# Square roots and rows of a first routing moved from GpSimd and VectorE to ScalarE, and two index layouts cut into smaller pieces

## The reference

```python
x = x + 0.5 * ffn(layernorm(x))          # first mixture of experts
x = x + attention(layernorm(x))          # 16 heads of 8 features, queries = keys = values
x = x + 0.5 * ffn(layernorm(x))          # second mixture, same weights

def ffn(x):                              # 8 experts, 128 -> 512 -> 128, two per token
    xf = layernorm(x) * ln_g + ln_b
    scores, idx = top_k(xf @ router_w, 2)
    gate = softmax(scores)
    # per expert: h = layernorm(xf) * eg + eb
    #             y = clip((h @ W1 + b1) * silu(clip(h @ W2 + b2))) @ Wo + bo
    return sum of gate * expert(xf)
```

## Time and profile before

| | us |
|---|---|
| median of 3 runs (1407.98, 1411.99, 3628.1) | 1411.99 |
| the profiled execution, its own time | 1400.55 |
| its span, from the first to the last instruction | 1398.8 |
| PE busy | 1254.7 (90%) |
| DVE busy | 1168.3 (84%) |
| ACT busy | 895.1 (64%) |
| POOL busy | 539.3 (39%) |

### The profile page before, as it was taken

One profiled execution on the slowest core, in us unless ns is written; L12 is line 12 of the kernel. 1 busy time (PEld: TensorE's weight loads), 2 busy tenths in 40 slices (PEclk: granted clock), 3 DMA queues, 4 the chain that ended last, 5 costly groups with the idle time before them and its releaser, 6 DMA issues.

```text
span 1398.8 us, 29592 instructions
## 1 busy us (share of the span) xinstructions
PE 1254.7 (90%) x10053; PEld 647.7 (46%) x10053; DVE 1168.3 (84%) x2329; ACT 895.1 (64%) x1881; POOL 539.3 (39%) x665
## 2 busy tenths in 40 slices
PE   3739999887789999999999999999998989999993
PEld 2737888775122222322323323223322238778882
DVE  8877888787978998889998888988898648988885
ACT  1214555554368888888778787788876875555651
POOL 3873557253442002334234424333432215643332
PEclk9999999999699999999999999999999999999996
DMA  8125654543303100112011021011100222555644
GB/s 267 41 69 186 222 204 179 214 177 103 83 21 88 37 25 15 36 37 72 19 45 51 10 58 37 23 32 52 36 2 19 87 96 94 196 181 200 235 169 161
DMA packets 65383, 135.58 MB, mean 97 GB/s; under 512 B 13330, under 2 KB 34932, under 8 KB 65204
## 3 DMA queue, kind: packets, MB, share of 16 engines
q1 hardware_dynamic: 56052, 115.39, 24.3%
q0 software_dynamic: 8704, 16.93, 3.8%
q10 hardware_dynamic: 480, 1.38, 0.3%
HBM read 47.35 MB, written 25.07 MB: 52 GB/s over the span
## 4 chain that ended last, share of the span: by engine, by line
PE 46%; DVE 18%; issue 3%; ACT 3%; POOL 3%; DMA 2%; SPq 1%; POOLq 0%; DVEq 0%; ACTq 0%
PE psum L2252 13%; DVE att_neg_part L1938 9%; PE psum L2228 8%; PE psum L2232 5%; PE psum L2209 5%; PE psum L2162 3%; PE psum L2150 3%; PE psum L2152 3%; DVE att_neg_part L1943 1%; ACT att_probs L1465 1%; DVE stats L1586 1%; PE psum L2275 1%; DVE ffn_x2c L1879 1%; ACT att_o_t L1480 1%; DVE ffn_hidden L1890 1%
## 5 line engine op out<-in xcount | busy, mean ns | idle before, releaser
L1465 ACT ACTIVATE att_probs<-psum 128x512 f32<-128x512 f32 x1024 | 556.5, 596 | 132.3 <-PE psum L2234 99.0
L1938 DVE TENSOR_REDUCE att_neg_part<-psum 128x2 f32<-128x1024 f32 x441 | 531.9, 1222 | 60.3 <-PE psum L2210 47.3
L2252 PE MATMUL psum<-att_probs,att_values 128*16 128x256 f32 x4096 | 323.8, 388 | 6.2 <-ACT att_o_t L1480 4.2
L1432 ACT ACTIVATE ffn_silu<-ffn_x2c,ffn_rec 128x256 f32<-128x256 f32 (+1 forms) x320 | 154.7, 487 | 173.0 <-DVE ffn_x2c L1879 171.5
L1289 POOL DMA_INDIRECT y_dram<-ffn_y,ffn_block_rows x144 | 143.4, 996 | 235.9 <-ACT ffn_y L1450 204.0
L2209 PE MATMUL psum<-att_right,att_left 64*128 64x512 bf16 x512 | 199.0, 389 | 13.4 <-DVE att_neg_part L1938 9.2
L2231 PE MATMUL psum<-att_right,att_left 64*128 64x512 bf16 x512 | 200.7, 392 | 8.9 <-DVE att_neg_part L1938 7.5
L2228 PE MATMUL psum<-att_right,att_left 64*128 64x512 bf16 x512 | 200.5, 392 | 6.6 <-DVE att_neg_part L1938 6.4
L2210 PE MATMUL psum<-att_right,att_left 64*128 64x512 bf16 x512 | 199.5, 390 | 0.0
L1879 DVE TENSOR_SCALAR ffn_x2c<-psum,ffn_rec 128x256 f32<-128x256 f32 (+1 forms) x320 | 162.5, 512 | 40.6 <-PE psum L2152 36.7
L2232 PE MATMUL psum<-att_right,att_left 64*128 64x512 bf16 x512 | 195.7, 382 | 0.0
(11 more groups left out here) (218 smaller groups left out, 1543.3 us busy)
## 6 DMA issues: line engine op xcount, KB each, us to landing
ffn_rec<-record SPq DMA_DIRECT2D x80, 776.5 KB, 3.8
ffn_block_rows<-rows_dram SPq DMA_DIRECT2D x64, 130.0 KB, 3.1
att_left<-q_parts_dram SPq DMA_DIRECT2D x64, 96.0 KB
att_right<-q_parts_dram SPq DMA_DIRECT2D x124, 48.0 KB
record<-in_L_ffn_W SPq DMA_DIRECT2D x16, 256.0 KB, 6.6
last_y<-y_dram SPq DMA_DIRECT2D x6, 512.0 KB, 6.6
att_right<-q_parts_dram SPq DMA_DIRECT2D x92, 32.0 KB
y_dram<-ffn_y,ffn_block_rows POOLq DMA_INDIRECT x144
```

Of the source, the lines that this page charges most:

```text
L1465: S.activation(probs[:, slot % PROBS, :], ring_bank(("score", slot))[:, :], ACT.Exp, scale=SCALE).then_inc(att_bank.by_act, 1)
L1938: last = V.tensor_reduce(out=neg_part[:, h % 2, keys, p::PAIR, t], in_=psum[:, low:high + 1, :], axis=AX.X, op=ALU.max, negate=True)
L2252: last = TE.matmul(value_bank[head * VS:head * VS + VW, q], values[:, b % 2, kt, team * TEAM + head, :], probs[:, (UNIT * n + j) % PROBS, ...
```

## The change

1. In the first routing (k_ffn == 0) POOL no longer does steps 1 and 6. ACT does them with Sqrt. DVE inverts what ACT left and puts a Newton step behind it (`vector_exact_scale`, four small instructions that wait for each other), twice per batch.
2. The rows of step 6 are written by ACT, 8 instructions of 128x256 with a scale and a bias per token; DVE makes the bias with one more small instruction. DVE's places (step 11) wait for the rows, by a semaphore.
3. ACT gets one-element activations (`warm`) that only load a function table early: Sqrt at the program's start and behind the exponential of batches 0, 1 and 2, Exp behind step 1 of batches 1, 2 and 3 and behind step 6 of batch 3.
4. The early layout of the second mixture is cut into 8 pieces, 3 slots apart, in place of 3 pieces 4 slots apart; the late one into 9 in place of 8, where the piece of six wide instructions becomes two. In the first mixture the same instructions run without a gap, as before.

```diff
@@ by_pool: which powers POOL still does
+            before = [j for j in JOBS if j[0] == 1 and set_of(j) is set_of(job) and j[4] < job[4]]
+            return set_of(job).by_pool, len(before) * POOL_STEPS + step
+        def roughly(job, which):
+            return 2 * job[1] + which
...
-                    plan_parts((at + 211, at + 215, at + 219), "lay", 0, 0)
+                    plan_parts(range(at + 211, at + 235, 3), "lay", 0, 0)
...
-        plan_tail(range(40, 56, 2), "lay", 1, 0)
+        plan_tail(range(40, 57, 2), "lay", 1, 0)
@@ pool_route
-            if step in (1, 6) and part[0] == 0:
+            if step in (1, 6) and part[0] == 0 and k_ffn == 1:
@@ scalar_program
+            S.wait_ge(pool_made, 4)
+            S.activation(warm[:, 2 * B + 1:2 * B + 2], euler[:, :], ACT.Sqrt)
@@ scalar_route
+            if k_ffn == 0 and step in (1, 6):
+                which = 1 if step == 1 else 2
+                S.wait_ge(*by_dve(job, SHIFTED1 if which == 1 else SHIFTED2))
+                S.activation(r.rstd[:, :], r.shifted[:, :], ACT.Sqrt).then_inc(rough_scale, 1)
+                if which == 2:
+                    S.wait_ge(*by_dve(job, FILLED))
+                    for t in range(nt):
+                        row = S.activation(r.rows[:, t, :, 0:F], r.xf[:, t, :].unsqueeze(1).to_broadcast([P, TOPK, F]),
+                                           ACT.Identity, scale=r.rstd[:, t:t + 1], bias=r.place_f[:, 1, t:t + 1])
+                    row.then_inc(rows_by_act, 1)
+                if b and which == 1 or b == B - 1:
+                    at = b + (b == B - 1 and which == 2)
+                    S.activation(warm[:, at:at + 1], euler[:, :], ACT.Exp)
...
                 S.activation(r.ratio[:, 0:nt], r.ratio[:, 0:nt], ACT.Exp).then_inc(r.by_act, 1)
+                if k_ffn == 0 and b < B - 1:
+                    S.activation(warm[:, B + 1 + b:B + 2 + b], euler[:, :], ACT.Sqrt)
@@ vector_route, step 2
-                V.wait_ge(*by_pool(job, RSTD1))
+                if k_ffn == 0:
+                    vector_exact_scale(job, 1)
+                else:
+                    V.wait_ge(*by_pool(job, RSTD1))
...
+            elif step == 6 and k_ffn == 0:
+                vector_exact_scale(job, 2)
+                V.scalar_tensor_tensor(r.place_f[:, 1, :], r.mean_var[:, :, 0], -1.0, r.rstd[:, :],
+                                       ALU.mult, ALU.mult).then_inc(r.by_dve, 1)
...
+        def vector_exact_scale(job, which):
+            r = set_of(job)
+            V.wait_ge(rough_scale, roughly(job, which))
+            step = r.place_f[:, 0, :]
+            settle(V.reciprocal(r.rstd[:, :], r.rstd[:, :]))
+            settle(V.tensor_tensor(step, r.rstd[:, :], r.rstd[:, :], ALU.mult))
+            settle(V.scalar_tensor_tensor(step, step, -0.5, r.shifted[:, :], ALU.mult, ALU.mult))
+            settle(V.scalar_tensor_tensor(r.rstd[:, :], step, 1.5, r.rstd[:, :], ALU.add, ALU.mult))
@@ vector_places
+            if k_ffn == 0:
+                V.wait_ge(rows_by_act, b + 1)
@@ vector_lay_out_early: 3 pieces become 8; vector_lay_out_late: 8 become 9
-            for at in share(part, 3):
+            for at in share(part, 8):
...
@@ vector_places_of_blocks: the last of its pieces is cut in two
-            else:
+            elif at == 2:
                 settle(V.tensor_reduce(out=whose[:, 0, some], in_=passed[:, some, 1:2 * E + 1], axis=AX.X, op=ALU.add))
                 settle(V.tensor_tensor(passed[:, some, 0:2 * E], passed[:, some, 0:2 * E], passed[:, some, 1:2 * E + 1],
                                        ALU.subtract))
+            else:
                 V.tensor_scalar(second[:, some], whose[:, 0, some], float(E), -float(E), ALU.is_ge, ALU.mult)
```

More of the change, by code:

```diff
@@ L187, in build_macaron @@
         euler = sbuf("euler", [P, 1])
-        warm = sbuf("warm", [P, 1])
+        warm = sbuf("warm", [P, 2 * B + 4])
         goes = sbuf("goes", [P, T, TOPK], I32)
@@ L367, in build_macaron @@
         pool_made = semaphore("pool_made")
+        rough_scale = semaphore("rough_scale")
+        rows_by_act = semaphore("rows_by_act")
         dve_made = semaphore("dve_made")
@@ L486, in by_pool @@
         def by_pool(job, step):
-            return set_of(job).by_pool, job[4] * POOL_STEPS + step
+            before = [j for j in JOBS if j[0] == 1 and set_of(j) is set_of(job) and j[4] < job[4]]
+            return set_of(job).by_pool, len(before) * POOL_STEPS + step
+        def roughly(job, which):
+            return 2 * job[1] + which
         def by_act(job, step):
@@ L1388, in scalar_experts @@
         def scalar_experts(k):
-            if k == 0:
-                S.wait_ge(pool_made, 4)
-            S.activation(warm[:, :], minus_half[:, :], ACT.Silu)
+            S.activation(warm[:, 2 * B + 2 + k:2 * B + 3 + k], minus_half[:, :], ACT.Silu)
             if k == 0:
@@ L1696, in vector_places @@
         def vector_places(job):
-            _, _, _, nt, _ = job
+            k_ffn, b, _, nt, _ = job
             r, few = set_of(job), slice(0, nt)
+            if k_ffn == 0:
+                V.wait_ge(rows_by_act, b + 1)
             settle(V.tensor_tensor(r.place[:, few, :], r.tallies[:, 0, :, 1:nt + 1].rearrange("p e t -> p t e"),
@@ L1736, in vector_lay_out_early @@
                     settle(V.tensor_copy(firsts_i[:, :], firsts_f[:, :]))
+                elif at == 1:
                     V.tensor_scalar(firsts_i[:, :], firsts_i[:, :], BLOCK.bit_length() - 1, None,
@@ L1742, in vector_lay_out_early @@
                     settle(V.tensor_copy(firsts_f[:, :], firsts_i[:, :]))
+                elif at == 2:
                     vector_pairs(0, EARLY)
+                elif at == 3:
                     V.tensor_tensor(taken[:, :], got[:, 0:E], got[:, E:2 * E], ALU.add)
@@ L1747, in vector_lay_out_early @@
                     settle(V.tensor_scalar(skipped[:, 0, :], skipped[:, 0, :], float(BH), None, ALU.mult))
-                else:
-                    vector_places_of_blocks(at, 0, 1)
-                    if at == 2:
-                        vector_whole_places(0, 1)
+                elif at < 7:
+                    vector_places_of_blocks(at - 3, 0, 1)
+                else:
+                    vector_whole_places(0, 1)
         def vector_lay_out_late(part=WHOLE):
-            for at in share(part, 8):
+            for at in share(part, 9):
                 if at == 0:
@@ L1789, in vector_lay_out_late @@
                                                   ALU.mult, ALU.add))
-                elif at < 7:
+                elif at < 8:
                     vector_places_of_blocks(at - 4, 1, len(SECTIONS))
```

## The result

The changed kernel takes **1432.65 us** (median of 4 runs, 1432.04 to 1434.82) against 1409.99 for the kernel before, run beside it: a ratio of **1.0176, 95% interval 1.0158 to 1.0195**. 1417 was forecast, 1405 to 1428. The profiled execution took 1432.94 us, its span is 1431.2.

The account below looks back on a forecast made before the run. POOL's and DVE's chains bound the first 107 us, PE from the fourth slice on. First routing +11.1 and layouts -5.9 gave +5.2: 1405.8 on the profiled execution, 1417 at the median, range 1405 to 1428.

Parts of the forecast that it names:

- the part on the roots: First routing: ACT's step 6 root stands behind two folds' scalings, free 15.1 us after the first turn; 11.7 in batch 3.
- the ledger: First routing's times summed batch by batch: second product at 129.6 instead of 118.55, +11 us, bounds +7 and +14.
- root at 33.4 + 15.1 = 48.5: Batch 1 of the first routing: PE's turn at 33.4, ACT's root 15.1 us later, comparisons at 49.8 against 41.09.
- the 11 us: Delay of the first block's second product, +11 us, all of it reaching the end because PE is the bound behind it.
- The bottom line: Whole kernel: +11.1 from the first routing and -5.9 from the layouts make +5.2 us on the profiled execution.
- ACT's rows: First routing, step 6: eight 128x256 rows on ACT take 3.7 us per batch; bounds 2.3 and 9.2.
- rival 3: First routing: ACT's rows cost 1.17 us each instead of 0.45, 23 us more, +28 in all, 1440; chance 0.04.
- rival 4: First routing: each table load stops ACT another 1.28 us before the tally's copy, four batches, +5.1, 1422; chance 0.05.
- The layouts: Second mixture: smaller pieces save PE 3.3 us at the early layout, 2.6 at the late one; -5.9, bounds +2 and -10.
- Rival 1: Layouts: smaller pieces give nothing back because DVE is full in the attention; +11 to +13, 1424; chance 0.18.
- Rival 2: First routing: folds do not hold ACT's root, second product about 8 us earlier than before, median 1398; chance 0.08.
- Carried to the median: Whole kernel: profiled execution of before lies 11.4 us below the 1411.99 median, so forecast 1405.8 becomes 1417; chance 0.60.

Follow-up runs that it names:

- chip D: Set of runs on one chip: the changed kernel, unaltered, took 1403.06 us against 1393.61 for the kernel before, ratio 1.0061.
- chip A: Set of the result, chip not recorded: the changed kernel, unaltered, took 1432.65 us against 1409.99 for the kernel before, ratio 1.0176.
- C: Set of runs on one chip: the changed kernel, unaltered, took 1427.46 us against 1402.66 for the kernel before, ratio 1.0183.
- F: Set on one chip: changed kernel 1.0053 of the kernel before; with folds behind the root 0.9973; with idle POOL powers too 0.9955.
- B: Set on one chip: kernel before 1395.40 us, with small layout pieces alone 1391.33; changed kernel with old pieces 1406.66, ratio 1.0074.
- E: Set on one chip: kernel before 1409.04 us; changed kernel with idle POOL powers 1413.75, with 0.2 us POOL products instead 1422.10.

## Why the prediction was wrong

Where PE starts a matmul, less where it started the same one in the trace of before, in us; the columns are its place in that trace (the early layout lies between 1054 and 1082, the late one between 1230 and 1275):

```
                       125      245       410        1054      1082      1230     1275     1370
forecast               +11.1                         +11.1     +7.8      +7.8     +5.2     +5.2
changed, chip D        +11.1    +11.8     +10.2      +10.4     +7.1      +7.1     +5.5     +5.8
changed, chip A        +28.1    +33.2     +31.9      +32.6     +29.3     +34.7    +32.5    +32.8
layout pieces alone    +0.1     +0.1      -1.0       -0.9      -4.6      -3.0     -4.7     -4.7
old pieces, chip D     +11.1    +11.8     +11.4      +11.6     +10.3     +10.5    +9.1     +9.7
```

1. **The step that failed** is in the part on the roots and the ledger's "root at 33.4 + 15.1 = 48.5", taken from a trace in which every product reached ACT when PE had it. It took the delay from PE's end to ACT's start as a constant, and it is not: on A it was 2.7, 3.5 and 6.2 us for the logits of the three batches and up to 9.3 for the folds. The first root came 55.09 - 48.18 = 6.9 us later than on D, the second 14.0 and the third 16.9, and 16.9 is what the second product is late beyond the ledger.
2. The same happens in the mixtures: between the changed kernel's traces on A and on D, the 16.9 us grow to 22.1 within the first 80 us of the first mixture and to 27.8 behind the gap at 1223. The kernel before has its share of this on C (against the trace of before it stands at -0.9 at 125 and at +2.7 at 245), so only part of it is the change's.
3. The ledger itself was right, shown on D and F: DVE's waits to 0.7 us, PE's turns to 0.8 (32.63, 60.47 and 94.73 against 33.4, 60.9 and 95.2), the second product to 0.1. So was the statement that the 11 us are still there at the early layout, within 1 us on D; on F 8.2 were left of them there, of which no run shows why. The bottom line was less right: against the kernel before in the same set the change costs 9.45 us on D and 6.66 on F, not 5.2, and 22.7 on A and 24.8 on C. The traced execution of before, 1400.55, lies 5 to 7 us above the medians of B, D and F without a late release, and why is not known.
4. ACT's rows took 4.04 us per batch, 3.7 forecast; rival 3 (1.17 us each) fell. The table load is a row of 1.28 with the next activation at most 1.30 behind its start, nine times over; rival 4 fell. The Trainium skill, "ScalarE: Activation LUTs", *What ACT_TABLE_LOAD costs*, has a drain of 1.38 us beside the load; in none of these nine does ACT stand still for it.
5. The layouts: -5.9 forecast; -5.4 alone and -4.9 inside the change on D. Early -3.3, as forecast; late -1.6 instead of -2.6. Rival 1 fell, the clock held at 1.00. But the old pieces, in the changed kernel on D, give -1.3 and -1.4 at the same places, so only some 2 us of it, all at the early layout, are the pieces' own there. The forecast took the stalls of the earlier trace rows as fixed, while a kernel shifted by 11 us meets them in another phase.
6. Rival 2's order was real as an experiment, but its price was not: with the folds out of the root's way the second product comes 3.3 us earlier than before, not 8, as PE's folds and ACT's table load then stand ahead of the tally.
7. Carried to the median: 1400.55 + 5.2 became 1417 by adding the 11.4 us between the profiled execution and the median. Those 11.4 us were the one sign ahead of the result that some executions of this program are slower than the traced one. I took them as a constant for both kernels. The sets without late releases had the kernel before at 1394 to 1395, those with them at 1403 to 1410. I should have asked what differs, and put a case for "what slows those runs strikes the new critical path too" among the rivals.

That a pause on POOL keeps releases in time rests on two executions on one chip (E), and the fold of 62.19 on C shows that one pause is not always enough. What on the chip delays them is not known: from 28 to 56 us the scatters' packets are 512 on A, C and D alike, of the same sizes, and took 102 to 103 ns each in the mean. That removing the powers is the whole cause on A and C was not tried there, nor whether the folds' order with powers beats the kernel before on such a chip.

## What to carry to other kernels

An engine's wait for another's product is not a constant of the program: before work is put behind a wait that nobody cared about, ask what a late release there would cost. Long runs of back-to-back indirect DMAs are suspect, and an operation of 1.7 us within them, which looks like pure loss, may protect the releases around it, as it seems to have done on E. When a trace lies well off the median of the runs, the traced execution may lack just the thing that the runs have; look at more than one set of runs before a forecast, or a verdict, of one per cent is believed.

## What was not expected of the hardware

- Releases came up to 9.4 us late in three sets of runs of six (A, C, E), and no row of the traces from B, D and F is remote; the changed kernel is the same in A, C, D and F. In the first routing the first one over 1 us late was due 6 to 10 scatters, some 8 to 14 us, behind POOL's last pause of 1.7 us or more. The Trainium skill, "Perfetto Trace Analysis", *Tensor Engine Instruction (MATMUL, LD_WEIGHTS)*, has the spread of a semaphore's update to all engines as a step of its own behind the reported end. No row here tells whether it is this step or one next to it that stretches.
- Late releases arrive together: two of PE's, due 3.4 us apart, within 0.16 us.
- In the same three sets the kernel before took 8 to 16 us more (1402.66 to 1409.99 against 1393.61 to 1395.40).
